# An attention and mixture-of-experts kernel: GpSimd's scatter list reordered, the last batch's routing moved to the first tile steps

## What is computed

```python
x = x + attn(layernorm(x), w_lhs, w_rhs)
x = x + ffn(layernorm(x), router_w, w_fc, b_fc, w_proj, b_proj)

def attn(x, w_lhs, w_rhs):
    scores = einsum('nsd,ntd->nst', x * w_lhs, x * w_rhs)
    return einsum('nst,ntd->nsd', softmax(scores, axis=2), x)

def ffn(xf):                                  # xf: 4096 tokens x 128
    probs = softmax(xf @ router_w.T)          # 8 experts
    topk_probs, topk_idx = top_k(probs, 2)
    topk_probs /= sum(topk_probs)
    h = gelu(einsum('nc,ech->neh', xf, w_fc) + b_fc)     # hidden 512
    out = einsum('neh,ehc->nec', h, w_proj) + b_proj
    return einsum('nec,ne->nc', out, combine(topk_probs, topk_idx))
```

## Time and profile before

| | |
|---|---|
| median of 3 timed runs | 371.75 us (371.2 to 372.22) |
| the profiled execution's own time | 370.49 us |
| span of its instructions | 368.7 us |
| busy: PE, PE weight loads | 293.3 us (80%), 256.7 us (70%) |
| busy: DVE, ACT, POOL | 222.1 us (60%), 194.5 us (53%), 185.7 us (50%) |
| mean granted TensorE clock | 0.92 |

### The profile page before, as it was taken

How to read it: one execution, slowest core, us unless ns; L and a number is a source line. 1 busy time by engine, 2 the same in 40 slices (tenths; PEclk the granted TensorE clock), 3 DMA queues, 4 the chain that set the end, 5 groups by cost and what they waited for, 6 DMA issues and landing times.

```text
span 368.7 us, 7888 instructions
## 1 busy us (share of the span) xinstructions
PE 293.3 (80%) x2206; PEld 256.7 (70%) x2207; DVE 222.1 (60%) x890; ACT 194.5 (53%) x392; POOL 185.7 (50%) x247
## 2 busy tenths in 40 slices
PE   8989988999769994999699272999999999995000
PEld 3669985889558883788588161999999999995000
DVE  3759788888837887778667022665544544453055
ACT  4445557862635614746588022677776777772000
POOL 7011034543865137488786675456555655566300
PEclk9999999999998999999989776799999999999555
DMA  7920000030010001014213321023322222111198
GB/s 218 431 95 1 2 1 0 3 117 16 22 51 29 4 16 45 29 32 118 75 38 90 81 75 59 30 74 110 89 81 75 80 80 72 45 37 50 48 338 325
DMA packets 16948, 29.37 MB, mean 80 GB/s; under 512 B 3760, under 2 KB 12848, under 8 KB 16656
## 3 DMA queue, kind: packets, MB, share of 16 engines
q1 hardware_dynamic: 12080, 18.40, 15.5%
q0 software_dynamic: 4832, 10.53, 8.6%
HBM read 16.30 MB, written 12.62 MB: 78 GB/s over the span
## 4 chain that ended last, share of the span: by engine, by line
PE 60%; DVE 15%; issue 11%; DMA 4%; POOL 4%; ACT 3%; another core or an unknown queue 2%; SPq 1%; POOLq 0%; ACTq 0%; DVEq 0%
PE av_ps L1295 18%; PE av_ps L1094 12%; DVE neg_piece L1402 6%; PE sc_ps L1276 5%; PE sc_ps L1274 5%; PE sc_ps L1275 5%; DMA raw_proj<-results 3%; PE bank L1262 3%; POOL results L867 2%; PE bank L1079 1%; PE sc_ps L1083 1%; PE bank L1083 1%; PE bank L1070 1%; DVE stats L1445 1%
## 5 line engine op out<-in xcount | busy, mean ns | idle before, releaser
L867 POOL DMA_INDIRECT results<-prob,result_row x78 | 75.2, 964 | 57.1 <-PE sc_ps L1276 35.3
L1295 PE MATMUL av_ps<-raw_proj,raw_fc 128*128 x624 | 80.9, 284 | 10.1 <-issue 10.1
L768 POOL DMA_INDIRECT slots<-stage,slot x64 | 63.1, 987 | 45.7 <-DVE stage L1562 21.9
L1295 PEld LDWEIGHTS av_ps<-raw_proj,raw_fc 128*128 128x128 f32 x624 | 76.8, 200 | 10.6 <-issue 9.9
L1011 ACT ACTIVATE raw_fc<-sc_ps,bfc,scale_down 128x256 f32<-128x256 f32 x156 | 75.3, 570 | 2.3 <-PE sc_ps L1276 2.3
L1094 PE MATMUL av_ps<-h_all,prob 128*128 128x137 f32 x512 | 73.2, 287 | 0.0
L1094 PEld LDWEIGHTS av_ps<-h_all,prob 128*128 128x128 f32 x512 | 67.3, 192 | 3.6 <-DVE res L1430 1.1
L1731 DVE TENSOR_TENSOR h_all<-av_ps,bpr 128x256 f32<-128x256 f32 x39 | 16.6, 425 | 75.3 <-PE sc_ps L1276 43.6
L1003 ACT ACTIVATE h_all<-bank 128x512 f16<-128x512 f16 x39 | 23.2, 597 | 60.1 <-PE sc_ps L1276 32.6
L1274 PE MATMUL sc_ps<-h_all,wfc_hi 128*128 128x256 f16 x156 | 43.7, 280 | 2.7 <-issue 1.8
L1275 PE MATMUL sc_ps<-h_all,wfc_hi 128*128 128x256 f16 x156 | 43.7, 280 | 1.1 <-issue 1.1
(11 more groups left out here) (177 smaller groups left out, 516.7 us busy)
## 6 DMA issues: line engine op xcount, KB each, us to landing
slots_in<-slots SPq DMA_DIRECT2D x39, 132.0 KB
raw_fc<-in_w_fc_dram SPq DMA_DIRECT2D x1, 2048.0 KB, 11.2
raw_proj<-in_w_proj_dram SPq DMA_DIRECT2D x1, 2048.0 KB, 15.4
raw_fc<-results SPq DMA_DIRECT2D x2, 1024.0 KB, 7.1
raw_proj<-results SPq DMA_DIRECT2D x2, 1024.0 KB, 11.7
out_dram<-res SPq DMA_DIRECT2D x4, 512.0 KB, 5.0
res<-in_x_dram SPq DMA_DIRECT2D x3, 512.0 KB, 5.6
results<-prob,result_row POOLq DMA_INDIRECT x78
```

The source lines that it names most:

```text
L768: pool.indirect_dma_start(out=slots[:, :], out_offset=bass.IndirectOffsetOnAxis(ap=slot[:, n, k:k + 1], axis=0), in_=stage[:, b % 2, t, :] ...
L867: pool.indirect_dma_start(out=results[:, :], out_offset=bass.IndirectOffsetOnAxis(ap=result_row[a][:, h:h + 1], axis=0), in_=gated[a][h], ...
L1295: mm = pe.matmul(o, hid[:, a % NH, c, s], wpr[:, e, c, :], start=(c == 0 and h == 0), stop=(c == HC - 1), skip_group_check=True)
```

## The change

POOL's list in the last batch's pass loses the paced waits: batch 1's scatters 5 to 11, `gate_powers(2)`, 12 to 15 and batch 2's 0 and 1 follow each other. After `scale_ln2(5)` come batch 2's 2 to 7 and the three `low_part`, and only then `gate_powers(3)`. The list in the tile stage begins with batch 2's scatter 8; two scatters stand between each of the other operations. DVE chooses all of batch 3 before the first tile step, PE ranks it in step 1 after `up(1)`, DVE keeps the ranks in step 1 and finds the slots in step 2; batch 3's scatters stand in steps 4 and 6.

```diff
--- before.py
+++ after.py
@@ -813,9 +813,14 @@
                     dispatch_max(b - 2)
                     dispatch_next(b - 2, 0)
                 if b == B - 1:
-                    dispatch_max(b - 2)
+
+                    for i in range(len(PACE_OWN), SCATTERS - 4):
+                        dispatch(b - 2, i)
                     gate_powers(ROUNDS_BY[b - 1] - 2)
-                    dispatch_next(b - 2, 0)
+                    for i in range(SCATTERS - 4, SCATTERS):
+                        dispatch(b - 2, i)
+                    for i in range(2):
+                        dispatch(b - 1, i)
                 if b >= 1:
                     scale_ln2(2 * b - 1)
                 if b == 1:
@@ -824,13 +829,15 @@
                     clear_empty()
                     for half in range(2):
                         store_empty(half)
-                if b >= 2:
+                if b == 2:
                     dispatch_next(b - 2, 1)
-                if b >= 1:
-                    gate_powers(ROUNDS_BY[b - 1] - 1)
                 if b == B - 1:
+                    for i in range(2, SCATTERS // 2):
+                        dispatch(b - 1, i)
                     for i in range(EMPTY_PIECES, PIECES):
                         low_part(i)
+                if b >= 1:
+                    gate_powers(ROUNDS_BY[b - 1] - 1)
                 if b >= 1 and b + 1 < B:
                     dispatch_own(b - 1, 0)
                 if b == 0:
@@ -844,20 +851,20 @@
                 if b >= 1 and b + 1 < B:
                     dispatch_own(b - 1, 1)
 
-            for i in range(5):
+            for i in range(8, 10):
                 dispatch(B - 2, i)
             scale_ln2(2 * B - 2)
-            for i in range(5, 11):
+            for i in range(10, 12):
                 dispatch(B - 2, i)
             scale_ln2(2 * B - 1)
-            for i in range(11, 15):
+            for i in range(12, 14):
                 dispatch(B - 2, i)
             gate_powers(len(ROUNDS) - 1)
-            for i in range(15, SCATTERS):
+            for i in range(14, SCATTERS):
                 dispatch(B - 2, i)
 
 
-            LAST_SCATTERS = {6: range(0, 8), 7: range(8, SCATTERS)}
+            LAST_SCATTERS = {4: range(0, 8), 6: range(8, SCATTERS)}
 
             def give_back(k, a):
 
@@ -1279,11 +1286,7 @@
             def down(k, a, of, last):
                 e = of
                 pe.wait_ge(gelu_done, k + 1)
-                if isinstance(k, int) and k == 0:
-
-                    pe.wait_ge(res_made, 2 * B)
-                    pe.wait_ge(lgpart_made, 2 * B)
-                if isinstance(k, int) and k == 3:
+                if isinstance(k, int) and k == 1:
                     pe.wait_ge(ranks_kept, len(ROUNDS))
                 if later(k, 2):
                     pe.wait_ge(biased_made, k - 1)
@@ -1301,12 +1304,14 @@
                     turn_slots(k + 2, (a + 2) % NB)
                 if tile_there(k):
                     up(k, a)
+                if isinstance(k, int) and k == 1:
+
+
+                    pe.wait_ge(res_made, 2 * B)
+                    pe.wait_ge(lgpart_made, 2 * B)
+                    rank_round(len(ROUNDS) - 1)
                 if later(k, 2):
                     down(k - 2, (a - 2) % NB, expert[a - 2], not tile_there(k + 1))
-                if isinstance(k, int) and k == 4:
-
-                    pe.wait_ge(biased_made, 2)
-                    rank_round(len(ROUNDS) - 1)
 
             pe.wait_ge(w_split, PIECES)
             pe.wait_ge(wpr_in, 16)
@@ -1700,7 +1705,9 @@
             add_logits(2 * B - 1)
             late_table = make_table(dve, note, settle, 2)
             last = len(ROUNDS) - 1
-            choose = picks(last)
+            steps(picks(last), 2 * K * E)
+            take_stats2(2 * B - 1)
+            take_moments2(2 * B - 1)
 
             expert = {}
 
@@ -1740,20 +1747,15 @@
 
             def step(k, a):
 
-                if k == 0:
-                    take_stats2(2 * B - 1)
-                    take_moments2(2 * B - 1)
-                if 1 <= k < 4:
-                    steps(choose, (5, 5, 3)[k - 1])
-                if k == 3:
+                if k == 1:
                     find_gap(last)
+                    keep_ranks(last)
+                if k == 2:
+                    find_slots(last)
                     split_h2(2 * B - 2)
                 if k < 5:
-                    steps(second_table, (3, 4, 4, 2, 20)[k])
-                if k == 5:
-                    keep_ranks(last)
-                    find_slots(last)
-                if k == 7:
+                    steps(second_table, (3, 3, 3, 6, 20)[k])
+                if k == 6:
                     split_h2(2 * B - 1)
                 if 8 <= k < 13:
                     steps(late_table, (5, 5, 5, 5, 20)[k - 8])
```

More of the change, by code:

```diff
@@ L826, in _ @@
                         store_empty(half)
-                if b >= 2:
+                if b == 2:
                     dispatch_next(b - 2, 1)
+                if b == B - 1:
+                    for i in range(2, SCATTERS // 2):
+                        dispatch(b - 1, i)
+                    for i in range(EMPTY_PIECES, PIECES):
+                        low_part(i)
                 if b >= 1:
                     gate_powers(ROUNDS_BY[b - 1] - 1)
-                if b == B - 1:
-                    for i in range(EMPTY_PIECES, PIECES):
-                        low_part(i)
                 if b >= 1 and b + 1 < B:
```

## The result

The kernel after takes 377.19 us (median of 4 runs, 374.43 to 377.92) against 371.48 us for the kernel before on the same chip (4 runs): ratio 1.014, 95% interval 1.008 to 1.020. It is **slower by 5.7 us**; the forecast was 3.9 us faster (from its median of 371.5 to 367.6), and the measured time lies outside the range. The profiled execution took 377.76 us, span 376.0, where the one of before took 370.49 and 368.7. Of the runs told further down, one execution of `b1` (500.15 us) and three of `a5` (342.57, 498.5 and 1619.63 us) came out slow and are left out of the medians and ratios.

The account below looks back on a forecast made before the run. PE bounds the kernel, losing 16.2 us idle in two tile-stage holes blamed on signals held by unpaced scatters. +4.9 us at `down(2)` becomes -4.1 at `up(9)`: 370.49 - 4.1 = 366.4, plus 1.26 gives 367.6 us; range 362.5 to 376.0.

Parts of the forecast that it names:

- The late gate: Last attention pass: round 3's gate comes at 174.2, DVE waits 5.4 us, attention ends about 3.9 us later.
- the two terms: Attention's end: late gate (+3.9) and unpaced run of ten (+5.8) do not add; the end moves +5.8.
- The credit of 1.4 us: Attention's end: POOL is silent there, so DVE's 1.36 us idle before the last `add_attention` is won; it starts at 180.3.
- point (1): Expected profile: batch 1's scatters end by 158, batch 2's first eight stand before 170, round 3's gate near 174.
- The run of ten: Batch 1's unpaced scatters from 138.8 to 151.6: signals late from 146.4 to 152.2, costing 5.8 us (bounds 0 to 6.2).
- the run of six: Batch 2's scatters 2 to 7 after `scale_ln2(5)`, last attention pass: end at 169.8, no hold counted.
- more than about five or six: Rule inferred from the trace: a longer run of unpaced scatters holds back PE's signals until POOL pauses.
- the -9.0 us from `down(2)` to `up(9)`: Tile stage: +4.9 us at `down(2)` becomes -4.1 at `up(9)`, the middle of -6.4 and -1.8.
- runs of eight: Tile stage: after POOL's wait for `up(5)`, eight more scatters run from 212.6 to 222.7, after which `up(9)` can start.
- rival C: Order changes, time doesn't: holds depend on the number of scatters, holes stay 16 us; about 371.7 us, chance 0.15.
- Rival A: Tile stage: signals stay held through POOL's one pause, +4.9 at `down(2)` stays; 376.7 us, or 373 to 377; chance 0.30.
- Rival B: Pacing never mattered in the last batch; only the late gate counts, +2.5 at attention's end; 365.7 us, chance 0.15.

Follow-up runs that it names:

- b1: The changed kernel, whole, on a chip with signals in time: 341.79 us against 339.69 for the kernel before, ratio 1.005.
- a5: GpSimd's list of the change with the early gate, tiles of the kernel before, on a chip in time: 340.25 us, ratio 1.001 to before.
- c2: `c1` with the three low parts moved between `gate_powers(3)` and the six scatters, held chip: 378.37 us against 371.42 for before, ratio 1.019.
- d4: Kernel before with a pause ahead of each four of the last batch's scatters in the tile stage, held chip: 376.80 us against 369.76, ratio 1.018.
- d3: `a4` with three pauses in the runs of ten and six scatters, held chip: 378.49 us against 369.76 for the kernel before, ratio 1.023.
- a4: The change with `gate_powers(3)` back ahead of the six scatters and low parts, chip in time: 338.17 us against 339.56 for before, ratio 0.997.
- c3: The changed kernel again, on a held chip: 376.45 us against 371.42 for the kernel before, ratio 1.016.
- c4: `a4` (the change with the early gate) on a held chip: 375.97 us against 371.42 for the kernel before, ratio 1.013.
- a2: Tiles of the change with GpSimd's list of the kernel before, chip in time: 343.94 us against 339.56 for before, ratio 1.012.
- a6: `a4` with the last batch's scatters at tiles 6 and 7 as before, chip in time: 342.69 us, ratio 1.010 to the kernel before.
- c1: `a5` with all sixteen scatters of the last batch at tile 6, held chip: 376.06 us against 371.42 for the kernel before, ratio 1.013.

## Why the prediction was wrong

**What held.** TensorE's signals are late where scatters follow each other without a gap, on the chips that do this at all: `c2` moved a run and its hold, `d4` cut holds with pauses, `d3` has none left in the attention stage. The late gate was absorbed, as I had it (the two terms do not add). The credit of 1.4 us at the attention's end came: DVE starts 0.05 us after the last `attend` where it started 1.5 after it before. `down(2)` was to lose 0.5 us more than the attention's end and lost 0.03 more (9.65 against 9.62). Batch 1's scatters end by 158, as in point (1). Where no signals are held, the gate's wait is 5.54 us on DVE and 3.67 on PE, near the 5.4 and 3.9 of the prediction. The median of `a4` lies 3.6 us under `b1`'s, on another chip; by their ratios it is 2.9.

**What was luck.** The run of ten was to cost 5.8 us and PE stood 5.85. But it was to do so in the run, from 7.6 us after its start. Signals passed in time for 10.7 us of that run (the last at 149.32); the hold came with the gate's short gap and the four scatters behind it, 153 to 159 and not 146 to 152. The size came out, the picture behind it did not.

**The first step that failed: the run of six, put at nothing.** I had the six scatters end at 169.8 with nothing waiting for a signal, and POOL silent afterwards. But the first hold also holds DVE, POOL waits 4.12 us for DVE's stage, and the six end at 173.02, in front of the last exponentials. That is a second hold, 3.3 us of PE. Behind it the granted clock is 0.83 and not 1.00, and the last 64 matmuls take 1.6 us longer. So DVE's last `add_attention` starts 5.85 + 3.3 + 0.3 + 1.6 - 1.5 = 9.6 us later (185.53 against 175.91; the 0.3 is what remains at the start of those matmuls), where I had 5.8 - 1.4 = 4.4. `c3` repeats both holds, shorter (PE stands 4.4 and 2.0 us) and without the slower matmuls (7.71 us, clock 1.00); there that start is at 183.46. `c4` sends the six later, and the second hold is gone. I had applied my own rule to the run of ten and not to the run of six.

The rule itself, "more than about five or six", does not hold as a count. In `d4` a signal is 1.6 us late behind four scatters. In `d3` six follow each other from 159.40 to 166.75 and hold nothing, and here ten passed signals for 10.7 us. What decides it stays open.

**The second: the -9.0 us from `down(2)` to `up(9)`.** I had +4.9 turn into -4.1. Measured, +9.65 turned into +6.9, a gain of 2.8. `down(2)` to `up(7)` took 18.2 us where I had 15.7 and before 19.2; `up(7)` to `up(9)` took 18.75 where I had 15.1 and before 20.5. I had counted on runs of eight. The results given back in between belong to the runs: twelve indirect DMAs follow each other from 197.86 and twelve more from 219.59, and the signals that are held before `up(9)` come 2.4 us after the second dozen (236.87 behind 234.52). The number that GpSimd owes is the same as before, which is what rival C said of this stage: its zero is nearer to the 2.8 than my 9.0.

The sum: 4.75 too little at `down(2)`, 6.2 too much won to `up(9)`, 0.4 behind it: 11.4 us, the difference between 366.4 and 377.76.

Rival A named the right result (373 to 377) with half of the right mechanism. Its condition came true, the last hole ended at 236.90, after 233. But its place was the tile stage with +4.9 from the start of the tiles, while the loss was made earlier, at the attention's end; the tile stage did win a little. Rival B, that the pacing never mattered, is what the chips in time show; but there the tile stage has no holes from which its gain was to come, and the change loses 2.1 us.

**The other failed assumption was silent.** Everything was worked out from one trace in which some 31 us (371.4 against 339.7) belong to the chip. Of the 27.1 us by which `up(9)` starts later there in the kernel before (233.08 against 205.98), 22.7 lie in the tile stage. Neither kind makes the change faster: slower by 5.0 and 5.7 us where signals are held, by 2.1 where they are not.

**No version beats before on both.** The change with the early gate (`a4`, `c4`) is the best in time, 0.3% faster than before on its chip, and 1.3% slower on the held ones.

## What to carry to other kernels

A wait that paces GpSimd's scatters may be there for the engines that listen to TensorE: before taking it out, look at how long the run without a gap becomes, what stands right behind it, and redo the list's times with the first delay in them, since a run that was to be over early slides into the next critical signal. When a step is moved ahead of a gate, price the gate's waiter (5.54 us here), and keep the two halves of such a change apart: where signals were in time, the earlier scatters won and the late gate lost more. And time a schedule on more than one chip before believing that its holes are the kernel's.

## What the runs showed of the hardware

- The same program took 339.6 to 340.1 us on some chips and 369.8 to 371.5 on others, each within 1%. On the slow ones TensorE's signals were raised late while GpSimd issued indirect DMAs 1.27 us apart. Some came 1.1 to 1.4 us after the run's end or a pause's beginning, in the tile stage 2.1 to 2.4 us after the run's end (212.62 behind 210.54 in the kernel before, 236.87 behind 234.52 in the kernel after), and some inside a run (221.59 in the kernel before, 157.08 in the kernel after). On the others more than 50 of them in a row from 189.4 us on (`a2`) held nothing.
- Why the chips differ is not shown. One more difference is on record: the traces of held chips have 2525 to 2768 semaphore events, those in time 4581 to 4668, though every kernel issues the same 142 indirect DMAs. Up to 80 us the counts agree; the first indirect DMA starts at 89. What is missing is mostly the landings of DMAs. So it is not excluded that the recording of such events has a part in the holds; no run tests it.
- On the held chips a gap of 1.0 to 1.1 us after every second indirect DMA, as in the steady tile stage from 243 us, is enough to keep PE full: it is busy 101.23 of 102 us there.
- In the holes PE itself trickles: in the kernels before and after single matmuls of `down` start 1.4 to 2.8 us apart with "issue" as releaser. Whether the held signals and this trickle are one thing stays open.
- A VectorE `tensor_scalar` of 0.17 us took 3.03 to 3.10 us beside GpSimd's three low parts (`a4`, `a5`, `a6`, `c1`, `c4`).
